# Fourier steps moved behind the chunks of the next convolution, and the first image pair normalised in place in both its copies, in a four-layer convolution and FFT kernel

## The reference, cut to what matters

```python
x = _L0_conv_ref(x, ...)              # a 3x3 convolution, softmax weights, a 3x3 local filter
for j in range(4):
    z = conv3x3(x, Kj)
    z = batchnorm(z, gamma[j], beta[j]); z = relu(z)
    z = conv3x3T(z, Kj)               # same kernel, transposed and flipped
    x = x + 0.1 * z
    x = batchnorm(x, gamma[j], beta[j])
    Bh = fft2(Lj padded)              # one 3x3 kernel per channel
    t = 1 / (0.1 * abs(Bh)**2 + 1)
    x = real(ifft2(fft2(x) * t))
```

## Time and profile before

| | us |
|---|---|
| median of 3 runs | 698.69 |
| lowest and highest of them | 698.69, 700.88 |
| the profiled execution's own time | 700.2 |
| its span, first to last instruction | 698.4 |
| from one layer's first table matmul to the next one's (310.17 to 446.97) | 136.8 |

### The profile page before, as it was taken

How to read it: one execution, slowest core, us unless ns; L and a number is a source line. 1 busy time by engine, 2 the same in 40 slices (tenths; PEclk the granted TensorE clock), 3 DMA queues, 4 the chain that set the end, 5 groups by cost and what they waited for, 6 DMA issues and landing times.

```text
span 698.4 us, 14578 instructions
## 1 busy us (share of the span) xinstructions
PE 619.7 (89%) x5840; PEld 200.9 (29%) x5840; DVE 493.7 (71%) x875; ACT 343.7 (49%) x640; POOL 233.3 (33%) x180
## 2 busy tenths in 40 slices
PE   6498999999999979999898899998978989989783
PEld 4122333222332223233232222332222223323221
DVE  2679888865786785738868767486778554867674
ACT  1466666652894322419932314299223233982232
POOL 0367666771142432202225222022252220222200
PEclk9699999999999999999999999999999999999988
DMA  9995111117600022294000224930004159000044
GB/s 187 182 168 97 32 32 33 31 31 161 157 1 1 1 63 62 70 224 116 1 2 1 70 55 107 224 79 1 2 1 109 30 133 218 3 2 1 1 123 120
DMA packets 44786, 51.21 MB, mean 73 GB/s; under 512 B 36528, under 2 KB 36656, under 8 KB 42672
## 3 DMA queue, kind: packets, MB, share of 16 engines
q1 hardware_dynamic: 40240, 48.99, 32.8%
q10 hardware_dynamic: 4480, 1.30, 1.2%
HBM read 11.99 MB, written 4.19 MB: 23 GB/s over the span
## 4 chain that ended last, share of the span: by engine, by line
PE 54%; ACT 20%; DVE 14%; issue 6%; DMA 3%; SPq 1%; POOL 0%; DVEq 0%; ACTq 0%; POOLq 0%
PE psum L1025 29%; ACT Z L613 10%; PE psum L1097 6%; ACT work L635 6%; PE psum L1164 3%; PE psum L1048 3%; DVE Z L950 2%; DMA X<-X 2%; PE psum L1221 2%; PE psum L1193 2%; PE psum L1236 2%; DVE work L923 2%; PE psum L1085 2%; DVE work L968 2%; DVE work L933 1%
## 5 line engine op out<-in xcount | busy, mean ns | idle before, releaser
L1025 PE MATMUL psum<-X,wts 128*32 128x512 f32 x1536 | 171.3, 594 | 9.1 <-DMA X<-X 5.0
L1025 PE MATMUL psum<-Z,wts 128*32 128x512 f32 x1536 | 172.3, 594 | 4.3 <-DVE Z L890 4.3
L474 POOL TENSOR_TENSOR Z<-X 128x512 f32<-128x512 f32 x64 | 80.8, 1286 | 251.2 <-DVE X L908 251.2
L635 ACT ACTIVATE work<-X,small 128x512 bf16<-128x512 f32 x128 | 90.7, 710 | 87.7 <-DVE X L908 87.7
L550 ACT ACTIVATE Z<-psum 128x512 f32<-128x512 f32 x64 | 38.2, 596 | 140.4 <-PE psum L1025 129.3
L484 POOL TENSOR_TENSOR X<-Z 128x1024 f32<-128x1024 f32 x24 | 56.9, 2394 | 113.0 <-DVE Z L950 113.0
L810 DVE BATCH_NORM_STATS2 stats<-Z 128x6 f32<-128x512 f32 x60 | 41.0, 691 | 69.7 <-ACT Z L550 69.6
L1025 PEld LDWEIGHTS psum<-Z,wts 128*32 128x32 f32 x1536 | 50.1, 109 | 115.5 <-issue 106.9
L613 ACT ACTIVATE Z<-Z,small 128x512 f32<-128x512 f32 (+4 forms) x92 | 80.3, 922 | 5.2 <-DVE small L880 4.7
L1025 PEld LDWEIGHTS psum<-X,wts 128*32 128x32 f32 x1536 | 47.8, 109 | 121.4 <-issue 109.8
L908 DVE SCALAR_TENSOR_TENSOR X<-psum,X 128x512 f32<-128x512 f32 x64 | 44.2, 690 | 36.2 <-PE psum L1025 36.0
(11 more groups left out here) (127 smaller groups left out, 819.5 us busy)
## 6 DMA issues: line engine op xcount, KB each, us to landing
X<-X SPq DMA_DIRECT2D x64, 260.0 KB, 3.9
Z<-Z SPq DMA_DIRECT2D x32, 520.0 KB, 9.2
Z<-x SPq DMA_DIRECT2D x36, 128.0 KB, 4.1
out<-Z SPq DMA_DIRECT2D x24, 128.0 KB, 2.4
parS<-par SPq DMA_DIRECT2D x4, 673.0 KB, 11.8
Z<-x SPq DMA_DIRECT2D x12, 120.0 KB, 5.1
Z<-x ACTq DMA_DIRECT2D x14, 64.0 KB, 4.3
Z<-x SPq DMA_DIRECT2D x14, 64.0 KB, 4.7
```

Source lines behind the costliest of these rows:

```text
L474: nc.gpsimd.tensor_tensor(rows(Z0, REG, bp, CH * (2 * half + i), CH), low, high, op=op)\
L635: nc.scalar.activation(by_row(rest[:, o:o + N // 2].bitcast(bf16)), xc, what, bias=small[:, 26:27], accum_out=sums[:, NCH * i + c:NCH * i ...
L1025: last = nc.tensor.matmul(out_b[C * r:C * r + C, :], weights[:, o:o + C], rows(src, reg, bp, g, CH, dj - 1), start=(dj == 0), stop=(dj == ...
```

## The change

It has five parts.

1. The first pair. Its X2 is filled by DMA as soon as GpSimd has written X0, before the norm is known. Then the norm is applied to both: ScalarE scales X0 in three pieces and the two border rows of X2 (`scale_first`), VectorE scales the rest of X2 in three pieces (`scale_copy`, between the two halves of pair 1's `move_back`). conv1's chunks 0 to 2 wait for these pieces.
2. The list. In the layers before the last, slot0c moves one chunk later, invH of pair 1 comes ahead of fwdW of pair 2, and slot0 and fwdH of pair 2 go from conv2's chunk 15 to around the norm, with invW of pair 1 ahead of it. slot0c and invH of pair 2 and fwdW of pair 3 move behind conv1's chunks 0, 2 and 3, and the stages of pair 3 behind chunks 5, 6 and 7 instead of 1, 3 and 5. The last layer keeps its own end (`last_steps`).
3. ScalarE's sums of x follow a table (`SUMS`) that delays some of them.
4. The weights of conv1 are made behind conv2's chunk 13, those of conv2 stay at "weights".
5. GpSimd's `unmix_halves` of a pair is reached at the second half of `back`, and its work on the fourth pair is described as not waiting for the norm.

```diff
+        9: [("slot0c", j, 0)] + fourier(j, 1, "fwdW"),
         10: fourier(j, 0, "invH"),
         11: fourier(j, 1, "fwdH"),
+        12: [("slot0c", j, 1)] + fourier(j, 0, "invW") + [("back", j, 0, 0), ("back", j, 0, 1)],
+        13: fourier(j, 1, "invH"),
+        14: fourier(j, 2, "fwdW"),
...
+    if j + 1 == DEPTH:
+        return steps + last_steps(j)
+    steps += quarters("fwdH", j, 2, (0, 1)) + [("slot0", j, 2), ("scaled", j, 2, 0)] + fourier(j, 1, "invW")
+    steps += [("moments", j), ("norm", j, 2)] + quarters("fwdH", j, 2, (2, 3))
+    steps += [("affine", j, 0), ("copied", j, 0), ("back", j, 1, 0), ("copied", j, 1), ("back", j, 1, 1), ("copied", j, 2)]
+    steps += [("scaled", j, 2, 1), ("turn", j, BP - 1), ("weights", j)]
     rest = {
-        0: [("affine", j, 1)],
-        1: fourier(j, 3, "fwdH"),
-        2: fourier(j, 2, "invW") + [("back", j, 2)],
-        3: fourier(j, 3, "invH"),
-        5: fourier(j, 3, "invW") + [("back", j, 3), ("affine", j, 2)],
+        0: [("slot0c", j, 2)],
+        2: fourier(j, 2, "invH") + [("affine", j, 1)],
+        3: fourier(j, 3, "fwdW"),
+        4: fourier(j, 2, "invW") + [("back", j, 2, 0), ("back", j, 2, 1)],
+        5: fourier(j, 3, "fwdH") + [("affine", j, 2)],
+        6: [("slot0c", j, 3)] + fourier(j, 3, "invH"),
+        7: fourier(j, 3, "invW") + [("back", j, 3, 0), ("back", j, 3, 1)],
         9: [("affine", j, 3)],
     }
...
+SUMS = {c: (c,) for c in range(5)} | {6: (5,), 8: (6,), 9: (7,), 10: (8,), 11: (9, 10), 12: (11,), 13: (12, 13), 14: (14,), 15: (15,)}
...
+            def scale_first(j):
+                for h in range(2):
+                    act.wait_ge(x2_in[0][h], 32 * (j + 2))
+                for g, n in ((0, CH), (CH, CH), (2 * CH, 2 * CH)):
...
+            def scale_copy(j, i):
+                dve.wait_ge(bn_ready, 2 * j + 2)
+                for h in range(2):
+                    dve.wait_ge(x2_in[0][h], 32 * (j + 2))
+                g, n = ((1, CH), (1 + CH, CH), (1 + 2 * CH, G - 1 - 2 * CH))[i]
+                z = rows(X2, REG2, 0, g, n)
+                nc.vector.tensor_scalar(z, z, S(12), S(13), ALU.mult, ALU.add).then_inc(copy_scaled, 1)
...
                         elif at[1] == 13 and j + 1 < DEPTH:
                             sum_kernels(j + 1)
+                            prepare((0,))
...
+                if j and c < 3:
+                    pe.wait_ge(x_back, NCH * (j - 1) + (1, 2, 4)[c])
+                    pe.wait_ge(copy_scaled, 3 * (j - 1) + c + 1)
```

More of the change, by code:

```diff
@@ L122, in fourier @@
     if what == "fwdH":
-        steps = [("slot0", j, bp)] + steps + [("slot0c", j, bp)]
+        steps = [("slot0", j, bp)] + steps + [("scaled", j, bp)]
     return steps
@@ L132, in layer_steps @@
         8: fourier(j, 0, "fwdH"),
-        9: fourier(j, 1, "fwdW"),
+        9: [("slot0c", j, 0)] + fourier(j, 1, "fwdW"),
         10: fourier(j, 0, "invH"),
         11: fourier(j, 1, "fwdH"),
[L136 to L139, removed]
+        12: [("slot0c", j, 1)] + fourier(j, 0, "invW") + [("back", j, 0, 0), ("back", j, 0, 1)],
+        13: fourier(j, 1, "invH"),
+        14: fourier(j, 2, "fwdW"),
     }
@@ L145, in layer_steps @@
         steps += after.get(c, [])
-    steps += [("moments", j), ("norm", j, 2), ("affine", j, 0), ("turn", j, BP - 1), ("weights", j)]
-    steps += fourier(j, 1, "invW") + [("back", j, 1)] + fourier(j, 3, "fwdW") + fourier(j, 2, "invH")
-    rest = {
-        0: [("affine", j, 1)],
-        1: fourier(j, 3, "fwdH"),
-        2: fourier(j, 2, "invW") + [("back", j, 2)],
-        3: fourier(j, 3, "invH"),
-        5: fourier(j, 3, "invW") + [("back", j, 3), ("affine", j, 2)],
+    if j + 1 == DEPTH:
[4 more added lines that the diff above has]
+    steps += [("scaled", j, 2, 1), ("turn", j, BP - 1), ("weights", j)]
+    rest = {
+        0: [("slot0c", j, 2)],
[5 more added lines that the diff above has]
+        7: fourier(j, 3, "invW") + [("back", j, 3, 0), ("back", j, 3, 1)],
         9: [("affine", j, 3)],
@@ L156, in layer_steps, with last_steps @@
     for c in range(NCH):
-        if j + 1 < DEPTH:
-            steps.append(("conv1", j + 1, c))
-        steps += rest.get(c, [])
-    return steps
+        steps += [("conv1", j + 1, c)] + rest.get(c, [])
+    return steps
+def last_steps(j):
+    steps = fourier(j, 2, "fwdH") + [("slot0c", j, 2), ("moments", j), ("norm", j, 2), ("affine", j, 0), ("turn", j, BP - 1)]
+    steps += fourier(j, 1, "invW") + [("back", j, 1, 0), ("back", j, 1, 1)] + fourier(j, 3, "fwdW") + fourier(j, 2, "invH")
+    steps += [("affine", j, 1)] + fourier(j, 3, "fwdH") + [("slot0c", j, 3)] + fourier(j, 2, "invW")
+    steps += [("back", j, 2, 0), ("back", j, 2, 1)] + fourier(j, 3, "invH") + fourier(j, 3, "invW")
+    return steps + [("back", j, 3, 0), ("back", j, 3, 1), ("affine", j, 2), ("affine", j, 3)]
+SUMS = {c: (c,) for c in range(5)} | {6: (5,), 8: (6,), 9: (7,), 10: (8,), 11: (9, 10), 12: (11,), 13: (12, 13), 14: (14,), 15: (15,)}
 ORDER = prologue_order()
@@ L169, in number_banks @@
     for step in steps:
-        if step in number or step[0] in ("turn", "back", "affine", "moments", "weights"):
+        if step in number or step[0] in ("turn", "back", "affine", "moments", "weights", "scaled", "copied"):
             continue
@@ L294, in build @@
         parts_added = sem("parts_added")
+        copy_scaled = sem("copy_scaled")
         rows_turned = sem("rows_turned")
@@ L489, in _ @@
                         mix_halves(j, at[1] // Q, at[1] % Q - 2)
-                    elif what == "back" and j + 1 < DEPTH:
-                        unmix_halves(*at)
+                    elif what == "back" and j + 1 < DEPTH and at[2] == 1:
+                        unmix_halves(*at[:2])
         @block.scalar
@@ L647, in scale_x @@
                     act.wait_ge(bn_ready, 2 * j + 2)
+                    if j + 1 < DEPTH:
+                        scale_first(j)
+                        return
                 for h in range(2):
@@ L657, in scale_x @@
                     nc.scalar.activation(dst, src, ACT.Identity, bias=small[:, 13:14], scale=small[:, 12:13]).then_inc(x_back, 2)
+            def scale_first(j):
+                for h in range(2):
+                    act.wait_ge(x2_in[0][h], 32 * (j + 2))
+                for g, n in ((0, CH), (CH, CH), (2 * CH, 2 * CH)):
+                    parts = [(X0, REG, g, n, 0, 128)]
+                    if g == 0:
+                        parts.append((X2, REG2, 0, 1, 2 * C, 128))
+                    if g + n == G:
+                        parts.append((X2, REG2, G, 1, 0, 2 * C))
+                    for t, reg, first, many, p0, p1 in parts:
+                        z = rows(t, reg, 0, first, many, 0, p0, p1)
+                        last = nc.scalar.activation(z, z, ACT.Identity, bias=small[p0:p1, 13:14], scale=small[p0:p1, 12:13])
+                    last.then_inc(x_back, n // CH)
             for j in range(DEPTH):
@@ L671, in _ @@
                             relu_pair(j, 3)
-                        sum_x(*at)
+                        for c in SUMS.get(at[1], ()):
+                            sum_x(j, c)
                     elif what == "slot0c":
@@ L698, in sum_kernels, with prepare @@
                                              op=ALU.add, axis=AX))
-            def prepare():
-                for k in range(2):
+            def prepare(some):
+                for k in some:
                     for form in range(2):
@@ L838, in _ @@
                     sum_kernels(0)
-                    prepare()
+                    prepare((0, 1))
                     gamma_and_beta()
@@ L978, in _ @@
                         dve.wait_ge(bn_ready, 2 * j + 2)
-                        prepare()
+                        prepare((1,))
                         gamma_and_beta()
@@ L998, in _ @@
                     elif what == "back":
-                        for half in range(2):
-                            move_back(*at, half)
-                    elif what == "slot0":
+                        move_back(*at)
+                    elif what == "copied":
+                        scale_copy(*at)
+                    elif what == "scaled":
                         if at[1] == 0:
                             dve.wait_ge(table_done, 4 * (j + 1))
-                        scale_slot0(*at)
-                    elif what == "fwdH":
-                        scale_fwdH(*at)
+                        if len(at) == 2:
+                            scale_slot0(*at)
+                        for h in at[2:] or (0, 1):
+                            for q in (2 * h, 2 * h + 1):
+                                scale_fwdH(j, Q * at[1] + q)
+                        if at[2:] == [0]:
+                            scale_slot0(j, at[1])
                     elif what == "conv1":
@@ L1186, in forward_h @@
                 first, q = NUMBER["fwdH", j, c], c % Q
+                if q == 0:
+                    pe.wait_ge(rows_moved, Q * (BP * j + c // Q + 1))
```

8 lines of the change are left out of this document (6 added, 2 removed).

## The result

| | before | after |
|---|---|---|
| median, 4 runs each on one chip, us | 699.4 (698.69 to 700.88) | 706.65 (705.76 to 707.55) |
| span of the profiled execution, us | 698.4 | 705.6 |
| its mean granted clock | 0.969 | 0.967 |

The changed kernel takes 1.0101 of the time before, with a 95% interval of 1.0075 to 1.0126: it is slower, by 7.3 us or 1%. The forecast was 701.5 with a range of 690 to 707, worked out from a median before of 698.7.

The account below looks back on a forecast made before the run. The layer was taken as a chain in which TensorE and VectorE take turns, no engine full. 698.7 less 0.5 (three layers) and 2.3 (last layer) gave 695.9; clock drops of 5.6 made it 701.5 us, range 690 to 707.

Parts of the forecast that it names:

- conv2's phase: From conv2's start to the end of pair 0's move_back: the new order gains 2.0 us a layer.
- The weights behind chunk 13: prepare's two multiplications end with GpSimd's two unmix_halves instructions, a price of 2.6 us; TensorE waits 2.5 us at fwdW of pair 2.
- the harmless one: Third piece of X2 through at 387.7 if ahead of GpSimd, 390.2 if behind; wanted at 392.8, so no cost at either.
- The norm: Around the norm, up to conv1's chunk 0: a gain of 4.1 us a layer, with a 2.4 us gap before chunk 0.
- conv1's phase: conv1's chunks and the stages between them: a loss of 3.9 us a layer.
- the two waits named: In conv1's phase: 1.6 us before invH of pair 3 for keep_slot0, 2.0 us for VectorE's statistics, taps and transposes.
- The last layer: No weights to prepare and its old end, so the early gain stays: 2.3 us gained.
- GpSimd's part: GpSimd's last sum and difference before the norm's end: nothing gained, as it waits for an addition alone.
- The clock: Gaps of 2.5, 2.4 and 2.0 us a layer, nine in all: three to four drop the clock, 5.6 us.
- Gain of a layer: 4.1 less 3.9, 0.2 us: Each of three layers: the norm's gain less conv1's phase's loss, 0.5 us in all three.
- more falls of the clock or a late transfer: Rival: nearly every gap drops, or pair 1's DMA or X2's third piece comes late; 708 us, chance 0.06.
- the case of three to five falls: The forecast's own case, three to five clock drops in the layers' gaps: 700.9 to 704.5 us, chance 0.42.

Follow-up runs that it names:

- e1_weights9: Changed kernel with conv1's weights (kernel sums and two multiplications) made behind conv2's chunk 9 instead of 13; 699.72 us, 0.9985 of the kernel before.
- e10_weights_alone: Kernel before with only part 4 of the change, conv1's weights made behind conv2's chunk 13; 705.92 us, 1.0060 of the kernel before.
- e7_old_list: Part 1 of the change alone, with the list, sums and weights of the kernel before; 702.61 us, 1.0017 of the kernel before.
- e2_taps8: Changed kernel with prepare_taps behind conv1's chunk 8 instead of 6; 699.66 us, 0.9995 of the kernel before.
- e3_affine_late: Changed kernel with ScalarE's scaling of pair 2 behind slot0c of pair 3; 707.97 us, 1.0115 of the kernel before.
- the three edits: Changed kernel with conv1's weights behind chunk 9, prepare_taps behind chunk 8 and pair 2's scaling behind slot0c of pair 3; 689.75 us, 0.9846 of the kernel before.
- e11_by_dma: Changed kernel with part 1 undone, the first pair scaled in X0 and then copied to X2 by DMA; 727.81 us, 1.0396 of the kernel before.
- e5_warm: Changed kernel with eight extra unused matmuls in TensorE's gap before conv1's chunk 0; 707.06 us, 1.0082 of the kernel before.
- e9_three_warm: Changed kernel with the three edits and eight extra unused matmuls in the gap before conv1's chunk 0; 682.22 us, 0.9727 of the kernel before.

## Why the prediction came out

**conv2's phase** was right. fwdW of pair 1 starts 31.79 us behind conv2 (31.7 was said: 348.1 less 316.39), invW of pair 0 at 47.27 (46.8), both behind an addition of VectorE. Of the 2.0 us, 1.75 were there at the end of pair 0's move_back: 373.31 less 321.43 is 51.88, for 53.63 before and 51.6 in the sum.

**The weights behind chunk 13** were right in kind and near in size: 2.27 us for 2.5. e1_weights9 and e10_weights_alone show it from both sides. The reading of the earlier trace rows, that a small instruction of VectorE ends with the GpSimd instruction that it meets, held for L744, which ended at 378.25 where GpSimd's pair ended at 378.13. It does not hold for every instruction: the sum L734 took 1.19 us beside GpSimd and 1.17 us without (e1_weights9). The other way round is in the rows above: the third piece of X2 (L936) was 0.15 us ahead of GpSimd's L502 and took 0.77 us, for 0.81 at most with GpSimd idle (e7_old_list), and GpSimd's pair took 5.12 us, for 4.74 at 373.39. Of the two ends given for it, the harmless one held.

**The norm** came 0.6 us later than summed: the averaging matmul 67.67 us behind conv2's start, for 67.06. 0.4 of it is L894 at 387.75, which takes 0.55 us and ends at 388.30, where GpSimd's L492 ends at 388.27. In the kernel before it took 0.16 us, with GpSimd idle:

```profile
383.80 0.16 DVE L857 TENSOR_SCALAR small<-small 128x2 f32<-128x2 f32 x1
```

It ends with a GpSimd instruction, as L744 does, and I had not looked for that there. The gap before chunk 0 was 2.41 us, 2.4 were said, and it is ScalarE's.

**conv1's phase** had the two waits named, 1.41 and 2.22 us for 1.6 and 2.0, and no wait at chunk 4. From chunk 0 to chunk 12 it takes 51.1 us, 1.4 of them by the clock; the sum made it 49.1. So 0.6 us a layer are missing from the sum. invW of pair 2 waits 0.2 us more (0.42 for 0.2) and chunk 12 0.4 us less (0.94 for 1.3), which leaves 0.8 us in small steps. Half of these follow from the prediction's own durations: a chunk takes 2.71 us before a stage and 2.57 before another chunk, and the new order has a stage behind seven chunks of this phase where the old one had it behind four, 0.4 us that the sum left out.

**The last layer** gained 1.7 us for 2.3. **GpSimd's part** changed nothing: its last sum and difference follow VectorE's addition in both kernels (385.75 in the rows above, 5.7 us ahead of the norm's end).

**The clock** was said to fall at three or four of nine gaps, and fell at four, three times before chunk 0 and once at invW of pair 3. By the rows these took 1.77, 1.38, 1.61 and 1.67 us, 6.4 together, for 5.6. The 1.7 us of a fall are half of the 3.50 us in which the earlier trace rows have the clock at 0.51. The gaps that the prediction calls always dropped are those of 2.58 us before the averaging matmul: in the kernel before, the clock fell to 0.50 behind all four, for 3.75 us (248.50 to 252.25, 385.00 to 388.75, 521.50 to 525.25) and in the last layer for 7 (665 to 672). The count was a guess, and that it came out is partly luck: the same gaps stood in e2_taps8 and e3_affine_late, and there other ones were hit.

**The size.** The forecast was 2.8 us more than before (701.5 for 698.7), and 7.3 us were measured. The term that was mis-sized is "Gain of a layer: 4.1 less 3.9, 0.2 us": without the clock the layers lost 1.3 and 1.1 us and gained 0.1, so 2.3 us were lost where 0.5 were to be gained. That is 2.8 of the 4.5 us between forecast and result; the clock is 0.8, the last layer 0.6, and 0.3 lie ahead of the layers. In the second layer the 1.2 us that are missing are the 0.6 of the norm and the 0.6 of conv1's phase above. The third layer gained only because the kernel before had its 2.67 us wait for a DMA there, which I left out; it is 0.98 us in the changed kernel. That the time still lies inside the range is in part luck: the range's upper end was set for more falls of the clock or a late transfer, the case of three to five falls ended at 704.5, and what carried the time past it was the error of the layers' sum. The 2.4% that the three edits then took off (706.65 to 689.75) came out of waits that the sum had named.

## What to carry to other kernels

Before a small instruction is moved into VectorE's idle time, look at what GpSimd does at that time: here 0.55 us of multiplications became 3 us and cost 7 us of time. When stages are moved so that they follow each other without work between, list for each engine's queue what stands between the stage's input and its output; a table build and a scaling did, the build for another 7 us, the scaling for 0.78 us a layer, which did not show in the time of its own experiment. A reordering that removes waits is worth its gain only when the new list's waits are looked up in the profile and taken out one by one: the same list went from 1% slower than before to 1.5% faster, and to 2.7% faster with the gap before chunk 0 filled as well.

## What the runs showed of the hardware

A granted clock of 0.50 came at or behind gaps of 2.2 to 2.7 us, but not at each: in the three layers of the changed kernel's profile at four of nine gaps of 2.22 to 2.42 us, in the kernel before behind all four of 2.58 us. Behind a gap of 2.67 us between two chunks the clock stayed at 1.00 (before, 574.82), and behind one of 2.66 us between the same two chunks it fell (e11_by_dma, 599.05, low from 600.00). With the 2.4 us gap before chunk 0 filled, the drops came at the others (e5_warm), and only with the other gaps gone did filling it pay (e9_three_warm, 7.5 us). So the price of a gap here was its own length and, at times, 1.4 to 1.8 us behind it, or 2.6 where the low clock lasted twice as long (chunk 0 at 533.80 in e3_affine_late, 5.35 us for 2.71). It also blurs small gains: e3_affine_late removed 0.8 us in each of three layers and was no faster. With the 6.75 us gaps of e11_by_dma the clock was low for 7.0, 7.25 and 10.5 us, from inside the gap on (395.00, where chunk 0 starts at 399.42).

Beside a GpSimd instruction, some small instructions of VectorE took longer and ended within 0.15 us of its end: of two multiplications of 128x96 the longer took 2.44 us, where two together take 0.55 without GpSimd (e1_weights9); a TENSOR_SCALAR of 128x2 took 0.55 for 0.16, and one of 128x32 2.26 for 0.24 (L724 in the earlier trace rows, and at 159.82 in the first layer before). The TENSOR_REDUCE of L734 took 1.19 us beside GpSimd and 1.17 without.
